# A fused attention and gated-MLP block: weight jobs issued ahead of the second stage's loads, and ScalarE issuing the query transfers

## The reference

```python
xn = _layernorm(x, axis=-1)
# attention s(xn)
qkv = jnp.clip(jnp.einsum('bsd,ed->bse', xn, Wqkv), -8, 8)
q, k, v = jnp.split(qkv, [512, 1024], axis=-1)
q, k = _layer_norm(q, q_ln_w, q_ln_b), _layer_norm(k, k_ln_w, k_ln_b)   # then 32 heads of 16
scores = jnp.einsum('bqhd,bkhd->bhqk', q, k) * 0.25 + slopes * rel
probs = jax.nn.softmax(jnp.where(causal, scores, -1e30), axis=-1)
s = jnp.einsum('bsd,ed->bse', jnp.einsum('bhqk,bkhd->bqhd', probs, v).reshape(B, S, 512), Wout)
# MLP: weights (int4 - zero) * scale, in groups of 128 rows; 512 -> 1792 -> 512
g = _silu(jnp.dot(jax.nn.silu(jnp.dot(xn, gate)) * jnp.dot(xn, up), down))
out = x + s * g
```

## Time and profile before

| | |
|---|---|
| median of the 3 runs | 1126.78 us |
| the profiled execution | 1119.51 us |
| its span, first to last instruction | 1117.7 us |
| mean granted TensorE clock | 0.978 of full speed |
| PE busy | 1039.0 us (93%) |
| DVE busy | 933.7 us (84%) |
| ACT busy | 722.6 us (65%) |
| POOL busy | 465.6 us (42%) |
| SP's DMA queue | 96854 packets, 93.72 MB |
| ACT's DMA queue | 1632 packets, 0.39 MB |

### The profile page before, as it was taken

How to read it: one execution, slowest core, us unless ns; L and a number is a source line. 1 busy time by engine, 2 the same in 40 slices (tenths; PEclk the granted TensorE clock), 3 DMA queues, 4 the chain that set the end, 5 groups by cost and what they waited for, 6 DMA issues and landing times. The chain is left out here.

```text
span 1117.7 us, 18980 instructions
## 1 busy us (share of the span) xinstructions
PE 1039.0 (93%) x6242; PEld 639.5 (57%) x6242; DVE 933.7 (84%) x2162; ACT 722.6 (65%) x1152; POOL 465.6 (42%) x554
## 2 busy tenths in 40 slices
PE   5999987998999999989999999899999999999995
PEld 4788764433344343433444333577778778777874
DVE  6778897887888787878889885579989998998896
ACT  3666655675767666666667668567747766774774
POOL 2566545221111111111121112039946864994686
PEclk9999999999999998999999999899999999999997
DMA  6254862543544544464454343100120011012001
GB/s 214 70 158 137 220 149 78 154 123 64 142 109 109 129 78 97 90 142 109 95 125 94 103 87 106 39 1 0 40 75 1 1 49 66 1 39 76 1 1 38
DMA packets 98584, 95.32 MB, mean 85 GB/s; under 512 B 28030, under 2 KB 80950, under 8 KB 98486
## 3 DMA queue, kind: packets, MB, share of 16 engines
q1 hardware_dynamic: 96854, 93.72, 32.7%
q10 hardware_dynamic: 1632, 0.39, 0.2%
HBM read 72.45 MB, written 21.23 MB: 84 GB/s over the span
## 5 line engine op out<-in xcount | busy, mean ns | idle before, releaser
L896 ACT ACTIVATE pr<-pair 128x1024 f32<-128x1024 f32 (+3 forms) x384 | 296.6, 813 | 168.1 <-PE pair L1017 90.7
L279 DVE CUSTOM_DVE_ANT_0 bank<-bank,sg 128x384 f32<-128x384 f32 (+3 forms) x488 | 231.4, 517 | 73.4 <-PE bank L289 72.1
L1538 PE MATMUL pair<-xc_lo,w_gu 128*128 128x512 f32 x448 | 182.6, 408 | 4.1 <-DVE xc_lo L1374 4.1
L1539 PE MATMUL pair<-xc_hi,w_gu 128*128 128x512 f32 x448 | 176.5, 394 | 0.0
L282 DVE TENSOR_REDUCE mx<-bank 128x1 f32<-128x512 f32 x240 | 150.5, 684 | 6.0 <-PE bank L289 3.7
L1386 DVE SCALAR_TENSOR_TENSOR gate<-pair,sgu,gate 128x512 f32<-128x512 f32 x168 | 124.5, 741 | 27.0 <-PE pair L1539 25.4
L1177 POOL TENSOR_TENSOR yt<-yt,tmp 128x512 f32<-128x512 f32 x96 | 124.2, 1314 | 0.0
L289 PE MATMUL bank<-ks,qs 108*128 108x512 bf16 (+3 forms) x384 | 116.2, 335 | 5.6 <-DMA ks<-in_krows 5.0
L1012 PE MATMUL pair<-s_sb,xin_c 111*128 111x512 bf16 (+3 forms) x384 | 97.8, 338 | 12.0 <-DMA s_sb<-dt 9.2
L289 PE MATMUL bank<-xin_c,s_sb 108*128 108x512 bf16 (+3 forms) x344 | 106.0, 341 | 3.1 <-DMA xin_c<-in_krows 3.0
L1012 PE MATMUL pair<-qs,ks 111*128 111x512 bf16 (+3 forms) x384 | 97.1, 337 | 12.7 <-DMA qs<-dt 11.0
(11 more groups left out here) (122 smaller groups left out, 2166.5 us busy)
## 6 DMA issues: line engine op xcount, KB each, us to landing
stk<-parts SPq DMA_DIRECT2D x16, 768.0 KB, 5.7
zst<-in_z_all SPq DMA_DIRECT2D x24, 448.0 KB, 4.0
sst<-in_w_all SPq DMA_DIRECT2D x24, 448.0 KB, 5.7
xin_c<-in_x SPq DMA_DIRECT2D x32, 256.0 KB, 3.3
s_sb<-stk SPq DMA_DIRECT2D x96, 64.0 KB
xin_c<-stk SPq DMA_DIRECT2D x96, 64.0 KB
qs<-stk SPq DMA_DIRECT2D x96, 64.0 KB
ks<-stk SPq DMA_DIRECT2D x96, 64.0 KB
```

The lines of the kernel that those rows point to most:

```text
L279: dve.tensor_tensor_reduce(out=src, in0=src, in1=tri[:, 512 - w:512], scale=1.0, scalar=-3.0e38, op0=ALU.add, op1=ALU.max, accum_out=dst). ...
L896: act.activation(pr[e % 3][:, 2 * p:2 * p + 2, 0:w], pair[p][:, :, 0:w], ACT.Exp, scale=SCALE)\
L1538: pe.matmul(GB[j % 4], w, xc_lo[:, k, :], start=True, stop=False)
L1539: pe.matmul(GB[j % 4], w, xc_hi[:, k, :], start=False, stop=True).then_inc(gu_done, 1)
```

## The change

In the second stage:

- `load` is split into `load_half` for queries (`which` = 0) and keys (`which` = 1). SP now issues the keys alone; ACT issues the seven query transfers of half 1 after `exps` of step 7 and those of half 0 after `exps` of step 11, for groups 0 to 13.
- SP's weight jobs: the first of a group is issued at the start of the group (for i = 0 it was issued ahead of the loop), and in odd groups a second one after it; both stand ahead of the loads and wait for `w_ready` as before.
- ACT converts at step 3 of every group and at step 8 of odd ones (`JOB_AT, JOB2_AT = 3, 8`); POOL's jobs move with it.
- The two loads of the first stage issue queries first and then keys, no longer alternating.

```diff
-        def load(sp, i, s, b, values=True):
-
+        def load_half(eng, i, s, b, which):
 
             cols = slice(b * 512, (b + 1) * 512)
             p0 = (i % 2) * 64
+            g = i % GROUPS
+            src = stk[which, bass.ds(i // GROUPS, 1), bass.ds(p0, 64), bass.ds(g // 2, 1), :, :]\
+                .rearrange("a (j c) k w s -> w c (a j) (k s)", j=GH)
             for r, both in enumerate(((0, 0), (1, 0), (2, 0), (0, 1), (1, 1), (0, 2))):
                 rows = slice(r * HD, (r + 1) * HD)
...
+                dst = (qs[s][rows, b, :, :], ks[s][rows, :, cols])[which]
+                eng.dma_start(dst, src[both[which]][:, :, cols]).then_inc(stk_in[s][b], 16)
+            extra, dst = ((qrows, qs[s][96:ROWS_MAX, b, :, :]), (krows, ks[s][96:ROWS, :, cols]))[which]
+            eng.dma_start(dst, extra[bass.ds(g, 1), :, :, cols].rearrange("a p j s -> (a p) j s")).then_inc(stk_in[s][b], 16)
+
+        def load(sp, i, s, b, values=True):
+            load_half(sp, i, s, b, 0)
+            load_half(sp, i, s, b, 1)
             if b == 0 and values:
                 load_v(sp, i, s)
...
-        JOB_AT, JOB1_AT = 6, 2
+        JOB_AT, JOB2_AT = 3, 8
...
                 def body(i, s, ip, last):
-                    if s == 1:
-                        half_job(ip, 2)
-                    if not last:
-                        half_job(*((ip, 1), (ip + 1, 0))[s])
-                    else:
+                    if i > 0:
+                        half_job(ip, s)
+                    if last:
...
+                    if s == 1:
+                        half_job(ip, 2)
                     if last is None:
 
                         sp.wait_ge(s_full[1], full(i, FIRST - 1, 1))
-                        load(sp, i + 2, s, 1)
+                        load_half(sp, i + 2, s, 1, 1)
 
                         sp.wait_ge(s_full[1], full(i, NSTEP - 1, 1))
-                        load(sp, i + 2, s, 0, values=False)
+                        load_half(sp, i + 2, s, 0, 1)
...
                 def body(i, s, ip, last):
-                    if s == 1:
-                        job(ip, 1)
-
                     pool.wait_ge(m_free, number(i, of_kind["own"][-1]) + 1)
...
                     chain(pool, mx0[:, :, :], 2 * i + 1)
-                    job(ip, (0, 2)[s])
+                    job(ip, s)
...
                         chain(pool, mx1[:, 0, :, :], 2 * i + 2)
+                    if s == 1:
+                        job(ip, 2)
...
-                        if e == JOB1_AT and s == 1:
-                            convert(ip, 1)
                         if e == JOB_AT:
-                            convert(ip, (0, 2)[s])
+                            convert(ip, s)
+                        if e == JOB2_AT and s == 1:
+                            convert(ip, 2)
                         exps(i, e, 0)
                         exps(i, e, 1)
+                        if last is None and e in (FIRST - 1, NSTEP - 1):
+
+                            load_half(act, i + 2, s, 1 if e < FIRST else 0, 0)
```

## The result

The changed kernel takes 1201.89 us, the median of 4 runs (1199.08 to 1206.48), against 1126.92 us of the kernel before in the same comparison: a ratio of 1.0669 (95% interval 1.0628 to 1.0711), 75 us slower. The forecast was 1179 us, in a range of 1150 to 1215.

What follows compares the result with a forecast made beforehand. PE was taken as the bound, its second-stage waits lying at group boundaries. Terms 13.3 + 25.1 + 14 − 10.2 + 10.5 = +52.7 us, set against the median 1126.78, gave 1179 us, range 1150 to 1215.

Steps and rivals of the forecast that it cites:

- ACT stands still while it issues: On ACT after steps 7 and 11: nothing behind an issue starts before it ends, 3.7 us for seven transfers.
- T: Time of a half's seven query issues on ACT, put at 3.7 us; the faster rival needed under 2.7 us.
- The stall behind it: PE late at step 9 behind ACT's issues: +13.3 us in seven even groups, +25.1 us in seven odd ones.
- The faster rival: ACT is not held up by issues, so boundaries shrink to 9.8 us: near 1089 us, chance 0.09.
- The boundary waits go: At group boundaries, PE's waits for `dt` and `krows` go, up to 28.2 us, with the clock's share.
- half had been counted: At the 14 boundaries, with PE idle 2.1 us each, a clock fall in half: 7 × 1.5 = +10.5 us.
- The clock at step 8: After PE's 3.6 us stall in odd groups the clock falls, +14 us; none counted in even groups.
- for the even groups' 1.9 us I count no fall: Even groups, step 9: PE's 1.9 us stall brings no clock fall; up to 7 × 1.5 us for the range.
- The bound of 1.80 us: PE idle time in a boundary window at which the clock stayed at 1.00, used to count no even-group fall.
- At the middle it is free: Weights for step 3's conversion landing in 5.7 us, the middle of 4.4 to 7.8, cost nothing.
- the forecast's own signs of being wrong: Step 8's `exps` starting while issues still run, boundaries of 10 us, or long waits for `z_in` at step 3.
- the second rival: Weights land late for step 3's conversion: PE loses 1.6 us in 15 groups, 24 us, about 1203 us; chance 0.13.

Runs made afterwards that it cites:

- e11: e9 with all seven query transfers of a half issued by ScalarE, none by SyncE: 1150.92 us, ratio 1.0230.
- e9: e4 with weight transfers placed where no small correction waits behind them, and GpSimd's first odd-group job ahead of its first chain of corrections: 1081.21 us, ratio 0.9591.
- e6: e3 with ScalarE issuing four query transfers of a half and SyncE the other three: 1112.33 us, ratio 0.9870.
- e4: e3 with ScalarE issuing only two query transfers of a half and SyncE the other five: 1108.39 us, ratio 0.9857.
- e3: The changed kernel with conversions at steps 5 and 10 in place of 3 and 8: 1165.10 us, ratio 1.0374.
- e1: The changed kernel with its weight jobs and conversions kept, but all query transfers back on SyncE: 1190.94 us, ratio 1.0588.
- e10: e9 with all query transfers issued by SyncE, none by ScalarE: 1086.37 us, ratio 0.9637.
- e5: The changed kernel with the first conversion moved from step 3 to 5, the second left at step 8: 1174.41 us, ratio 1.0420.

## Why the prediction was right, and where it was not

**ACT stands still while it issues: right.** T was forecast at 3.7 us from SP's rows; ACT's timeline shows 3.60 to 3.63 at 20 of the 28 places and 3.78 to 4.91 at the other eight. The stall behind it was forecast at 13.3 + 25.1 = 38.4 us for steps 7 to 11; PE's idle time there is 37.9. That the two agree so closely is in part luck: in the group shown the stall is 12.28 − 10.64 = 1.6 us where 1.9 was forecast, and the long issues, which the forecast does not have, make up the difference. That an instruction behind an issue starts only after it, taken from one place, holds at all 28 places (0.04 to 0.11 us after it), and e11 against e9 prices it alone at 69.7 us. The faster rival is out. e6 and e4 against e3 show how far ACT's idle time covers issues: four cost about as much as two, seven 53 us more than four. The rule that the time to initiate a transfer is usually small beside the transfer (the Trainium skill, page "DMA: Bandwidth & Descriptors", section "Issuing engines are not separate DMA queues") agrees with the first of these differences and not with the second.

**The boundary waits go: right.** `dt` and `krows` fell from 28.2 us to 1.8. Of the two reasons given, the place of the weights is enough: in e1 and e10, where SyncE issues all 14, PE's waits for these transfers are down to 3.5 and 2.4 us too. Where nothing else is late, a boundary takes 9.65 to 10.2 us (e9), forecast 9.8 for one without waits; with the seven issues 11.7 to 11.9 in half of e3's windows, forecast 11.9; in six of the 14 the clock falls, where half had been counted.

**The clock at step 8: too small.** The step "for the even groups' 1.9 us I count no fall" failed: the clock fell in all seven even groups as well, and PE's work from step 7 to 11 took 26.6 us longer where 14 had been counted. The bound of 1.80 us had been taken from a boundary, from a single stall. In e3, where the weights no longer stopped step 3, the even groups' step 8 ran without a fall, with the same stall (1.43 and 0.19 us); one of its windows from step 7 to 11:

```profile
284.96:295.77 10.81, 9.19 (x85) 4.39 (x84) 7.59 (x23) 5.80 (x9) 1.08 (x5) 1.00 0.66 85
```

PE's work takes 9.19 us there at full clock, where it took 8.8 before, so some 0.4 us a group of the 26.6 is not the clock. Why the clock fell in the one kernel and not in the other stays open.

**"At the middle it is free": wrong.** This is the term that was missing, and with it came one of the forecast's own signs of being wrong, long waits of the conversion at step 3 (29.1 us). The landing time of the weights was taken from transfers with less beside them: 5.7 us, 4.4 at best. Issued as early as forecast (5.2 us after step 11; forecast 5.0), they now shared the engines with keys, queries and values at once (DMA share of 0.87 and 0.76 in the boundary windows shown, against 0.45 to 0.64 in those of the earlier trace rows): 7.1 us in the middle, 8.7 at most. That the company makes them slow fits e1, where ACT issues no loads beside them and they land in 5.0, but no run changes it alone. The wait at step 3 is the second rival, which had a chance of 0.13, and it came beside the forecast's stalls, not in place of them: 27.5 us by e5, priced at up to 24 in advance. Its 1203 us is nearer to the measured 1201.89 than the forecast's 1179. That the range still holds the result is no luck: its high end had counted falls in the even groups (+10.5) and late weights in most groups (+15), and both came. 52.7 + 27.5 = 80, against 75 measured; what the clock adds behind the late weights is in these numbers and was not separated.

**The base.** The profiled execution of before (1119.51) is 4.9 us faster than any run of before in this comparison and that of after is the slowest of four (1206.48), so the two spans differ by 87 us where the medians differ by 75; runs of one kernel differ by 2 to 13 us.

## What to carry to other kernels

An issue of a transfer is work of the engine that issues it, though the profile counts it as idle time: put it against the idle time between that engine's instructions at that very place, one gap at a time, and split it (two or four, not seven) so that it fits. Before transfers are moved to a second engine to shorten the issue, look at what is queued in front of them: here the places of the weight jobs in the lists of SyncE, ScalarE and GpSimd were worth 41 us and the second issuer 5. And when several loads are made to start together, price each landing with all of them in flight.

## What the runs showed of the hardware

- Issuing one 64 KB transfer of 64 runs of 1 KB takes ACT as long as SP: six in 2.75 us on ACT, 0.46 each, and 0.83 for the 48 runs of `qrows` (SP: 0.47 and 0.92 in the earlier trace rows). Now and then one takes far longer: at 8 of the 28 places in the changed kernel the seven took 3.78 to 4.91 us in place of 3.6. No run shows why.
- A 12 KB transfer issued 0.29 us behind 896 KB on the other queue held PE until 6.0 us after its issue (e4, 241.46 to 247.50), against 2.25 us from issue to use with no loads and 3.3 us without a wait with the weights 6.3 us ahead (e9). The small transfer's own queue did not let it pass the large one.
- A stall of PE of 1.6 us in two pieces (1.44 and 0.19) let the clock fall in the changed kernel's even group shown (0.86 in its window); with the same 1.6 us in e3's it stayed at 1.00. Whether it falls is not settled by the length of the last stall alone.
